# A copy inside SBUF moved from VectorE to a DMA transfer, in an attention kernel

## The reference, cut to what matters

```python
xn = _layernorm(x)                                   # x: [8, 256, 512]
c_q, c_kv = xn @ Wq_down, xn @ Wkv_down              # latent 64
q_c = (c_q @ Wq_up);  k_c = (c_kv @ Wk_up);  v_c = (c_kv @ Wv_up)   # 128 heads x 4
q_r = (xn @ Wq_rope)                                 # 128 heads x 64
k_r = xn @ Wk_rope                                   # 64, shared by the heads
scores = (q_c k_c + q_r k_r) / sqrt(68)              # per batch and head, 256 x 256
s = softmax(scores) v_c @ Wo
g = silu(ffn(xn))                                    # 512 -> 1376 -> 512, tiled weights with low-rank parts
out = x + s * g
```

## Time and profile before

| | |
|---|---|
| median of three runs | 2008.1 us |
| profiled execution, its time | 2009.38 us |
| its span | 2007.5 us |
| mean granted TensorE clock | 0.991 |
| TensorE busy | 1953.1 us (97%) |
| VectorE busy | 1407.7 us (70%) |
| ScalarE busy | 1052.7 us (52%) |
| GpSimd busy | 496.2 us (25%) |
| transfers on the queue of SP | 22.4% of 16 engines' span |

### The profile page before, as it was taken

One profiled execution on the slowest core, in us unless ns is written; L12 is line 12 of the kernel. 1 busy time (PEld: TensorE's weight loads), 2 busy tenths in 40 slices (PEclk: granted clock), 3 DMA queues, 4 the chain that ended last, 5 costly groups with the idle time before them and its releaser, 6 DMA issues.

```text
span 2007.5 us, 38734 instructions
## 1 busy us (share of the span) xinstructions
PE 1953.1 (97%) x12448; PEld 1503.7 (75%) x12448; DVE 1407.7 (70%) x1654; ACT 1052.7 (52%) x1535; POOL 496.2 (25%) x798
## 2 busy tenths in 40 slices
PE   7799999999999999999999999999999999998998
PEld 5577777777777777777777777777777777765665
DVE  7688777676767676776767676767667676766555
ACT  5455555555555555555555555555555555552222
POOL 2345122222222121212121212222221212211222
PEclk9899999999999999999999999999999999998999
DMA  7411211121212121212121111112121212233331
GB/s 256 158 24 39 41 37 38 34 43 29 47 28 48 29 46 28 49 28 44 32 40 38 40 35 37 40 33 43 27 49 28 48 26 41 60 85 93 109 111 48
DMA packets 131723, 105.87 MB, mean 53 GB/s; under 512 B 52222, under 2 KB 96302, under 8 KB 131614
## 3 DMA queue, kind: packets, MB, share of 16 engines
q1 hardware_dynamic: 131678, 105.29, 22.4%
HBM read 51.76 MB, written 26.21 MB: 39 GB/s over the span
## 4 chain that ended last, share of the span: by engine, by line
PE 90%; DVE 4%; issue 1%; DMA 1%; ACT 1%; SPq 0%; POOL 0%; DVEq 0%; POOLq 0%; ACTq 0%
PE pj L905 34%; PE st L875 23%; PE sx L892 12%; PE ob L852 12%; PE ap L1469 3%; PE sx L860 1%; PE yp L1502 1%; PE zp L1502 1%; DVE mx L811 1%; DMA den<-r_scratch 1%; PE gp L1423 0%; PE zp L1455 0%; DVE slot L821 0%; DVE hid L1371 0%; DVE ol L1385 0%
## 5 line engine op out<-in xcount | busy, mean ns | idle before, releaser
L811 DVE TENSOR_REDUCE mx<-sx 128x4 f32<-128x1024 f32 x512 | 626.8, 1224 | 427.8 <-PE sx L892 410.1
L792 ACT ACTIVATE probs<-st 128x1024 f32<-128x1024 f32 x512 | 512.8, 1026 | 171.1 <-PE st L875 171.1
L762 ACT ACTIVATE slot<-pj 64x512 fp32r<-64x512 f32 x512 | 303.9, 594 | 434.4 <-PE pj L905 428.0
L712 POOL CAST k<-kc 64x512 fp32r<-64x512 f32 x256 | 169.3, 661 | 1026.1 <-PE st L875 1026.0
L875 PE MATMUL st<-slot,k 89*128 89x512 f32 x1024 | 417.8, 408 | 2.5 <-DMA slot<-mrow 1.3
L905 PE MATMUL pj<-xh,wh 128*128 128x512 f32 x1024 | 402.8, 393 | 4.4 <-PEq L217 3.3
L875 PE MATMUL st<-slot,krlh 128*128 128x512 f32 x1024 | 407.0, 397 | 0.0
L905 PE MATMUL pj<-xh,wl 128*128 128x512 f32 x1024 | 402.2, 393 | 0.0
L905 PE MATMUL pj<-xl,wh 128*128 128x512 f32 x1024 | 401.9, 392 | 0.0
L821 DVE TENSOR_TENSOR slot<-pj,slot 64x512 fp32r<-64x512 f32 x512 | 352.8, 689 | 16.1
L892 PEld LDWEIGHTS sx<-k,slot 88*128 88x128 f32 x2048 | 306.6, 190 | 69.7 <-issue 29.2
(11 more groups left out here) (171 smaller groups left out, 1340.1 us busy)
## 6 DMA issues: line engine op xcount, KB each, us to landing
w_stage<-in_Wq_rope SPq DMA_DIRECT2D x64, 256.0 KB, 3.1
c_scratch<-stage SPq DMA_DIRECT2D x32, 256.0 KB, 3.2
c_in<-c_scratch SPq DMA_DIRECT2D x128, 64.0 KB, 1.9
o_scratch<-o_sb SPq DMA_DIRECT2D x128, 64.0 KB, 2.1
k<-kc SPq DMA_DIRECT2D x128, 48.0 KB
slot<-kc SPq DMA_DIRECT2D x256, 24.0 KB
k<-kx SPq DMA_DIRECT2D x128, 48.0 KB
slot<-kx SPq DMA_DIRECT2D x256, 24.0 KB
```

The costliest lines, as they stand in the source:

```text
L712: nc.gpsimd.tensor_copy(k1[0:64, s, :, :].rearrange("p a n -> p (a n)"), krh[:, bp * CH:(bp + 1) * CH]).then_inc(k_ready, 1)
L762: nc.scalar.activation(slot1[0:64, (k - 1) % NS, e, :, :], pj[64 * e:64 * e + 64, :].rearrange("p (a n) -> p a n", a=2), ACT.Copy).then_in ...
L792: nc.scalar.activation(probs[:, k % NS, kt], st[:, kt], ACT.Exp, scale=SCALE).then_inc(exp_done, 1)
L811: nc.vector.tensor_reduce(mx[:, p, lo:lo + 4], sx[:, :, :].rearrange("p a (b k) -> p (a b) k", b=2), axis=AX.X, op=ALU.max).then_inc(red_d ...
```

## The change

The copy by VectorE is taken out. SyncE issues a transfer instead, 64 partitions of 4 KB each (256 KB), from `slot1[0:64, s]` to `slot2[0:64, s]`, once a step, after `qh_done` of that step. It stands in the body behind the max rows and ahead of the content loads. One semaphore for each slot (`s2_in[s]`) replaces `s2_done`, and TensorE's `scores` wait for it.

```diff
-        s2_done = sem("s2_done")
+        s2_in = [sem(f"s2_in{s}") for s in range(NS)]
...
+            def copy_hi(at, k):
+                s = k % NS
+                hold(sp, passed, qh_done, 2 * at.step(k) + 2)
+                sp.dma_start(slot2[0:64, s].bitcast(F32), slot1[0:64, s].bitcast(F32)).then_inc(s2_in[s], 16)
+
             def body(at, k):
                 if k % 2 and at.live(k - 3):
                     max_rows(at, k - 3)
+                if at.live(k - 1) and k <= STEPS:
+                    copy_hi(at, k - 1)
                 if at.live(k) and k < STEPS:
                     load_content(at, k)
...
                 if at.live(k - 1) and k <= STEPS:
-                    nc.vector.tensor_copy(slot2[0:64, s], slot1[0:64, s]).then_inc(s2_done, 1)
                     maxima(at, k - 1, 0)
...
                     pe.wait_ge(ql_done, 2 * v + 2)
-                    pe.wait_ge(s2_done, v + 1)
+                    pe.wait_ge(s2_in[s], 16 * (at.turn(k) + 1))
```

## The result

The changed kernel takes 2025.9 us (median of four runs, 2025.1 to 2026.4) against 2007.9 for the kernel before in the same comparison: a ratio of 1.0077, 95% interval 1.0064 to 1.0090. The medians lie 18.0 us apart; the ratio makes it 15.5 us, its interval 12.9 to 18.1. The forecast was 2025.0.

A forecast was written before the change was run, and what follows sets the result against it. TensorE's work, busy 97% of the span, was taken to bound the kernel. Content late 0.18 us times 111 pairs, 20 us, less 3.1 gained: +16.9 on 2009.4, less 1.3 to the median, 2025.0; 2003 to 2046 leaves about 0.15 out.

The forecast's parts named there:

- a wait on mrow: Sign of being wrong: a wait on the max rows' transfer (mrow) appears; a wait on the copy itself was another.
- SyncE's delay of content: Odd bodies: the copy's hold (0.23 us) and issue (0.52) between mrow and content start all three content transfers 0.75 later.
- The copy's packets in front of content: Odd bodies: the copy's data ahead of content on the DMA engines delays content 0.15 us, between 0 and 0.3.
- The margin: Time content is there before the even row scores' weight load: 0.87 us counted, 0.72 left after 0.15 for waits.
- The excess: Stall per pair of steps in the loop: 0.75 + 0.15 - 0.72 = 0.18 us, times 111 pairs 20 us.
- The last group: Last group of attention, 121st to 127th transpose, where SyncE also loads FFN small weights; the prediction had no loss there.
- VectorE's relief: Removing 256 copies, 180.3 us of VectorE: 0 in the loop, 3.1 us gained at attention's start and turn; bounds 0, 7.0.
- The turn: Turn to the FFN: removing the copy gives 0.69 us, because the last reading of o_scratch hangs on that chain.
- the likeliest case: Loop: content late by 0.08 to 0.35 us per pair; 2025 us, own range 2014 to 2038, chance 0.54.
- hidden anyway (a): Loop: the 0.75 us delay fits in the 0.87 margin, no stall, only the gain: 2005.0, range 2002 to 2014, chance 0.30.
- heavier case (b): Odd bodies: issue of 0.65 to 0.8 us and 0.3 queueing, 0.46 per pair: 2056, at worst 2074; chance 0.10.
- faster case (c): Attention's start and turn: VectorE's relief worth its full 7.0 us, copies there stretched by GpSimd, transfer hidden: 2001.1; chance 0.06.

The follow-up runs named there:

- content first: The changed kernel with the copy's transfer issued behind the three content transfers of a body, not ahead of them: ratio 0.9987 to the kernel before, which makes 2005 us.
- best order: Copy's transfer issued behind the content transfers; against that kernel, VectorE copies again in the last group for steps 0 to 14: ratio 0.9961 to the kernel before, 2001.6 us.
- even-body kernel: The changed kernel with the transfer in even bodies only, ahead of content, and VectorE's copy in odd ones: ratio 0.9978 to the kernel before, which makes 2004 us.

## Why the prediction was right, and where it was not

The mechanism held in the loop: no loss in even bodies, content late in odd ones, the copy itself and slot2 never awaited, the even-body row scores as the place. Two signs came otherwise. The profile names no landing for the wait, only "issue", and a wait on mrow, named as a sign of being wrong, stands in the last group (0.3 us). The total of 2025.0 against 2025.9 is in part luck: a loop put too dear by 5.4 us met a last group of 5.2 that was not counted. Term by term:

- **SyncE's delay of content**, put at 0.75 us: 0.72 measured (1.53 less 0.81, medians of the loop's 112 pairs).
- **The copy's packets in front of content**, put at 0.15: the last packet before the weight load starts 3.83 us behind content's first issue, before it was 3.81; by kind of pair 3.84 against 3.83 and 3.79 against 3.70. With 2 KB in the copy's place it is 3.84 and 3.81, so not even the 0.09 is the bytes'. This term was too large. The Trainium skill ("DMA: Bandwidth & Descriptors", "Queues, rings and completion order") says that each engine takes descriptors in ring order. The prediction's estimate from it, content 0.15 to 0.2 us behind the copy's packets and a sum the same or 5 us more, is not borne out by these runs.
- **The margin**, put at 0.72: 1.25 less 0.62 from last packet to weight load makes 0.63. The prediction had allowed 0.55 for what is 0.62. This term was too large too, by 0.09.
- **The excess**, 0.18 by the prediction: 0.72 + 0.02 - 0.63 = 0.11. These three terms add up to the load's delay by construction; the check from outside is the transposes, 0.13 a pair. The loop's loss was 14.6 us and not 20.
- **The last group** was missing. The tail's issues on SyncE are in the code; I counted the added issues there as free, since I read SyncE's slack only in the middle. It cost 5.2 us, some 1.5 of them by the lower clock behind a pause, and filled the gap that the 20 left.
- **VectorE's relief.** The turn gave 0.7 as put. The start gave 3.3 in the profiled execution where 2.4 stood. But the waits of TensorE's matmuls behind maxima fell only from 6.3 to 5.5 us there (those of its weight loads from 9.7 to 7.3), and the granted TensorE clock over 75 to 100 us was 0.81 in the execution after and 0.73 in the one before, so part of the 3.3 is the clock. How much is the relief stays open: kernels with the same code up to there (content first, best order) differ by 2.3 us.
- **In the loop** VectorE's relief was put at 0. It is 1.7 us without any copy and 3.4 in the even-body kernel, 0.02 and 0.03 us a pair. Which wait gives it I did not find.
- **The range** of the likeliest case doesn't fit its own bounds: 0.35 a pair would give 2005 + 39 = 2044, not 2038; 2038 belongs to 0.30. The result is inside either way.

Of the rivals, hidden anyway (a) is out, but narrowly: the margin was 0.63, the delay 0.72. By an estimate from the two kinds of pair, an issue 0.1 us shorter would have hidden it in one kind and 0.2 us shorter in the other. The heavier case (b) came in none of the 256 issues: they took 0.50 to 0.56 us, median 0.54. The faster case (c) is out: the copy was not hidden, and the kernel with no copy at all gains 6.6 us by its ratio. What (c) says of GpSimd is seen in part: its cast of k takes 607 ns where it took 656 (medians over the loop), and 656 still where VectorE copies in odd bodies. What that is worth no run separates. The operations of TensorE, VectorE and ScalarE got no longer in the loop: a matmul of pj has a median of 389 and 390 ns, a reduction to the maxima 1225 in both.

## What to carry to other kernels

A transfer has two prices: its bytes on the DMA engines and its issue on the queue that sends it. Where an engine works through a list of transfers in order, count the second and ask what stands behind it and when that is needed; here 0.7 us of hold and issue cost 0.13 us of TensorE at every second step, and moving one call behind another gave it back. Look for the fullest stretch of a queue, not the middle one (two pauses of TensorE there cost 5.2 us, clock included), and do not take a half-busy engine as a free place for an issue.

## What the runs showed of the hardware that was not expected

- The issue of a transfer inside SBUF by SyncE takes as long for 64 x 32 bytes as for 64 x 4096: median 0.54 us of 256 issues in both kernels. Sent directly behind another transfer, the small one took 0.58.
- 256 KB more per step on the DMA engines, 14.4 points more of DMA share, slowed no matmul that the chain shows (12 pj matmuls take 2.73 to 2.77 us before and after), and content's last packets came no later than with 2 KB in their place (3.83 us behind the issue in both).
- After a pause of 1.72 us TensorE ran with a granted clock of 0.58 over the next 3 us (mostly the level of 1.2 GHz), with 512-column matmuls 0.43 us apart and not 0.23. Behind one of 1.47 us in the same kernel the row scores took their usual 0.71.
- An issue on ScalarE's queue took 0.47 us and kept its activations apart by 0.62 where 0.21 stood before.
